# Attention stream: ScalarE exponentiates each head from the score banks, with the row maximum as bias, and sums in the same instructions

## The reference

```python
qp = q @ Wq.T
k, v = jnp.split(latent_kv @ Wkv_expand.T, 2, axis=-1)
scores = jnp.einsum('bhqd,bhkd->bhqk', qh, kh) * inv_sqrt_d
scores = jnp.where(causal, scores, jnp.finfo(scores.dtype).min)
attn = jax.nn.softmax(scores, axis=-1)
out = jnp.einsum('bhqk,bhkd->bhqd', attn, vh)
x = x + jnp.tanh(g_xattn[1]) * (out @ Wout.T)
```

## Time and profile before

| | |
|---|---|
| runs before, median (lowest to highest) | 2217.43 us (2213.9 to 2219.85) |
| the profiled execution | 2218.61 us |
| its span, first to last instruction | 2216.9 us |
| granted TensorE clock, mean | 0.942 |
| TensorE busy (matmuls) | 1946.2 us, 88% |
| VectorE busy | 1421.1 us, 64% |
| ScalarE busy | 959.1 us, 43% |
| GpSimd busy | 509.1 us, 23% |

### The profile page before, as it was taken

How to read it: one execution, slowest core, us unless ns; L and a number is a source line. 1 busy time by engine, 2 the same in 40 slices (tenths; PEclk the granted TensorE clock), 3 DMA queues, 4 the chain that set the end, 5 groups by cost and what they waited for, 6 DMA issues and landing times. The chain is left out here.

```text
span 2216.9 us, 33553 instructions
## 1 busy us (share of the span) xinstructions
PE 1946.2 (88%) x11866; PEld 1541.6 (70%) x11866; DVE 1421.1 (64%) x2759; ACT 959.1 (43%) x1983; POOL 509.1 (23%) x469
## 2 busy tenths in 40 slices
PE   1899999999499999999913999799959989999997
PEld 1677787777377777877711555466639879999996
DVE  3666666676666666666767777366664544666663
ACT  1333344443233333344465333355524425666663
POOL 3211010110311110001022000133220354565553
PEclk9999999999699999999956999899985999999999
DMA  5200000000321001000051000000013147777774
GB/s 135 74 6 33 37 37 37 37 1 1 76 74 38 2 35 37 37 37 1 1 227 63 0 0 0 1 1 1 1 61 98 40 126 166 236 237 232 230 238 99
DMA packets 39530, 154.61 MB, mean 70 GB/s; under 512 B 5472, under 2 KB 12848, under 8 KB 29050
## 3 DMA queue, kind: packets, MB, share of 16 engines
q1 hardware_dynamic: 27170, 128.39, 16.5%
q0 software_dynamic: 11408, 23.37, 5.8%
q10 hardware_dynamic: 840, 1.36, 0.2%
HBM read 132.59 MB, written 20.51 MB: 69 GB/s over the span
## 5 line engine op out<-in xcount | busy, mean ns | idle before, releaser
L608 DVE TENSOR_TENSOR la_q_roped<-banks,la_rope_q 128x400 f32<-128x400 f32 x384 | 197.9, 567 | 45.6 <-PE banks L400 28.6
L555 ACT ACTIVATE la_probs<-banks,la_minus_max 100x361 f32<-100x361 f32 x256 | 145.0, 566 | 157.2 <-DVE la_minus_max L643 157.2
L643 DVE TENSOR_REDUCE la_minus_max<-banks 100x1 f32<-100x361 f32 x256 | 135.7, 530 | 58.9 <-PE banks L426 52.1
L1751 DVE TENSOR_TENSOR ex_weights_low<-ex_raw_weights,ex_weights_high 128x2048 fp32r<-128x2048 f32 x60 | 137.4, 2290 | 51.2 <-ACT ex_weights_high L1658 48.5
L343 POOL TENSOR_TENSOR la_wq_high<-la_weights,zero 128x1024 fp32r<-128x1024 f32 x14 | 26.5, 1894 | 609.6 <-PE banks L372 609.6
L435 PEld LDWEIGHTS banks<-identity,la_probs 100*121 100x121 f32 x768 | 113.4, 184 | 64.3 <-DVE la_probs L650 29.6
L446 PE MATMUL banks<-la_probs_t,la_kv_rows 121*128 121x200 f32 x768 | 151.3, 333 | 0.0
L925 PE MATMUL banks<-qf_sign_weights,qf_x_quant_t 128*100 128x512 bf16 x512 | 122.9, 391 | 32.2 <-DVE qf_hidden L1006 18.1
L573 ACT COPY la_probs_t<-banks 121x300 f32<-121x300 f32 x256 | 106.2, 415 | 96.3 <-PE banks L435 96.3
L2007 POOL TENSOR_TENSOR ex_g_low<-ex_g,ex_g_high 128x256 fp32r<-128x256 f32 (+1 forms) x104 | 86.7, 949 | 232.6 <-ACT ex_g_high L1690 232.1
L435 PE MATMUL banks<-identity,la_probs 100*121 100x100 f32 x768 | 125.6, 272 | 16.0 <-DVE la_probs L650 14.5
(11 more groups left out here) (312 smaller groups left out, 5501.6 us busy)
## 6 DMA issues: line engine op xcount, KB each, us to landing
ex_raw_weights<-w_exp SPq DMA_DIRECT2D x60, 1024.0 KB
la_weights<-w_pack SPq DMA_DIRECT2D x16, 1984.0 KB, 7.8
qf_raw_weights<-w_ffn SPq DMA_DIRECT2D x2, 4096.0 KB
qf_raw_weights<-w_ffn SPq DMA_DIRECT2D x2, 2048.0 KB
out<-ex_block_out POOLq DMA_DIRECT2D x13, 256.0 KB, 4.4
residual<-x SPq DMA_DIRECT2D x1, 3200.0 KB
normed_rows<-ex_xn SPq DMA_DIRECT2D x16, 200.0 KB
out<-residual SPq DMA_DIRECT2D x4, 800.0 KB
```

Of the source, the lines that this page charges most:

```text
L555: act.activation(prob[:, s % 4, 0:L], ps[0:S, s % 2, 0:L], ACT.Exp, bias=nmax[:, s % 4:s % 4 + 1], accum_out=sums[:, s % 4:s % 4 + 1]).the ...
L608: dve.tensor_tensor(roped[:, h, v, c, :].rearrange("p (b s) -> p b s", b=GB), ps[:, B_BANKS[k % 2], 0:NT].rearrange("p (b s) -> p b s", b=GB),
L643: dve.tensor_reduce(nmax[:, s % 4:s % 4 + 1], ps[0:S, s % 2, 0:L], AX.X, ALU.max, negate=True).then_inc(s_max, 1)
L1751: dve.tensor_tensor(wl[:, m, :], raw[:, m, :], wh[:, m, :].bitcast(F32), ALU.subtract).then_inc(w_low[m], 1)
```

## The change

`less_max` becomes `least`: the maximum is taken with its sign turned, and nothing is subtracted. ScalarE's `exp` no longer works in place on SBUF but reads the score banks, one instruction for each head, with the negated maximum of this head as bias and with `accum_out`, which gives the head's row sum. VectorE's sum goes, and `sums` becomes `recips`. TensorE's `scores(j)` waits until the four heads of the item before have been exponentiated.

```diff
@@ TensorE, scores
                     if j >= 1:
-                        pe.wait_ge(s_sub, j)
+                        pe.wait_ge(s_exp, j * HPB)
@@ ScalarE
                 def exp(j):
-                    act.wait_ge(s_sub, j + 1)
-                    act.activation(p[:, j % PR, :], p[:, j % PR, :], ACT.Exp).then_inc(s_exp, 1)
+                    act.wait_ge(s_max, j + 1)
+                    if j >= PR:
+                        act.wait_ge(t_psum, j - PR + 1)
+                    if j >= 4:
+                        act.wait_ge(s_rec, j - 3)
+                    for h in range(HPB):
+                        act.activation(p[:, j % PR, h * S:(h + 1) * S], ps[0:S, h // 2, h % 2 * S:(h % 2 + 1) * S],
+                                       ACT.Exp, bias=mx[:, j % 4, h:h + 1],
+                                       accum_out=sm[:, j % 4, h:h + 1]).then_inc(s_exp, 1)
@@ VectorE
-                def less_max(j):
-                    four = "p b (h s) -> p b h s"
-                    banks = ps[0:S, 0:2, 0:2 * S].rearrange(four, h=2)
+                def least(j):
                     dve.wait_ge(s_psum, j + 1)
-                    dve.tensor_reduce(mx[:, j % 4, :].rearrange("p (b h) -> p b h", b=2), banks, AX.X,
-                                      ALU.max).then_inc(s_max, 1)
-                    dve.wait_ge(s_max, j + 1)
-                    if j >= PR:
-                        dve.wait_ge(t_psum, j - PR + 1)
-                    dve.tensor_tensor(p[:, j % PR, :].rearrange("p (b h s) -> p b h s", b=2, h=2), banks,
-                                      mx[:, j % 4, :].rearrange("p (b h) -> p b h", b=2).unsqueeze(3)
-                                      .to_broadcast([S, 2, 2, S]), ALU.subtract).then_inc(s_sub, 1)
-
-                def sums(j):
-                    dve.wait_ge(s_exp, j + 1)
+                    if j >= 4:
+                        dve.wait_ge(s_exp, (j - 3) * HPB)
+                    dve.tensor_reduce(mx[:, j % 4, :].rearrange("p (b h) -> p b h", b=2),
+                                      ps[0:S, 0:2, 0:2 * S].rearrange("p b (h s) -> p b h s", h=2), AX.X,
+                                      ALU.max, negate=True).then_inc(s_max, 1)
+
+                def recips(j):
+                    dve.wait_ge(s_exp, (j + 1) * HPB)
                     if j >= 4:
                         dve.wait_ge(s_norm, j - 3)
-                    dve.tensor_reduce(sm[:, j % 4, :], p[:, j % PR, :].rearrange("p (h s) -> p h s", h=HPB), AX.X,
-                                      ALU.add).then_inc(s_sum, 1)
-                    dve.wait_ge(s_sum, j + 1)
                     dve.reciprocal(rs[:, j % 4, :], sm[:, j % 4, :]).then_inc(s_rec, 1)
```

More of the change, by code:

```diff
@@ L1123, in causal_attention @@
         v_psum, v_out = sem("v_psum"), sem("v_out")
-        s_psum, s_max, s_sub, s_exp = sem("scores"), sem("scores_max"), sem("scores_less_max"), sem("scores_exp")
-        s_sum, s_rec, s_norm = sem("exp_sum"), sem("rsum"), sem("probs_normed")
+        s_psum, s_max, s_exp = sem("scores"), sem("scores_max"), sem("scores_exp")
+        s_rec, s_norm = sem("rsum"), sem("probs_normed")
         t_psum, t_out = sem("probs_t_psum"), sem("probs_t_out")
@@ L1420, in _ @@
                     if s < ITEMS:
-                        less_max(s)
+                        least(s)
                     if 1 <= s <= ITEMS:
-                        sums(s - 1)
+                        recips(s - 1)
                     piece = front_at(s - 1) if s else None
```

## The result

The changed kernel takes **2265.56 us** (median of four runs, 2260.77 to 2266.58) against 2217.72 before (median, now of four runs): ratio 1.0224, 95% interval 1.0204 to 1.0243. The forecast was 2264, range 2240 to 2282. The profiled execution has a span of 2263.6 us, 46.7 longer than before.

What follows compares the result with a forecast made beforehand. TensorE's work or a 2.26 us loop through the score banks was taken to bound each slot; the profiled 2218.6 us plus 26.3 (loop) plus 20.6 (clock) gave 2265.5, or 2264 in terms of the median, range 2240 to 2282.

Steps and rivals of the forecast that it cites:

- What bounds the kernel: Attention stream: a slot takes the longer of TensorE's own work or the scores-maximum-subtraction loop of 2.26 us.
- Four heads in the loop: ScalarE's four exponentials per slot enter the score-bank loop: 1.45 us together, lengthening it to 3.30 us.
- +26.3 us: Sum over the attention stream's slots of the longer loop's cost, at the clocks of before.
- the fall at 1616.5: Drop of the granted clock already in the stream before the change; 1.6 us, subtracted from the predicted clock loss.
- the clock term: TensorE's longer pauses in the stream make its clock fall to half more often: +20.6 us together.
- The accumulator reads: In ScalarE's heads, `accum_out` adds a 0.19 us read, with the next instruction 0.09 us behind its start.
- The row of the latent attention: Profile row of another stage: exponential of 0.56 us followed after 0.46, then a 0.19 us read; used to price heads.
- Removed work: On VectorE, 64 subtractions (in the loop) and 64 sums (beside the next slot, worth nothing) go: 72 us.
- four times 3.3: Last quarter: one clock fall per round, 2.5 us in the `out` slot plus 0.8 in a plain one.
- The held clock, the first rival: In the stream the clock holds as before, pauses being 2 us at most; only the loop counts, 2244; chance 0.2.
- Heads of another price: ScalarE's heads in the loop: short, about 2238, chance 0.08; long, 2280 without the clock, chance 0.1.
- The router stretch: Behind the stream, 49.6 us of half-clock TensorE work might meet another clock, at most 24.8 us shorter; chance 0.04.

Runs made afterwards that it cites:

- e4: The kernel before, with ScalarE exponentiating in SBUF in four instructions with accum_out and VectorE's sum gone, subtraction and its wait kept: 2227.01 us, ratio 1.0053.
- e2: The kernel before with one wait moved: scores wait for the exponential of the item before, not the subtraction; 2234.77 us, ratio 1.0088.
- e6: The changed kernel with two pairs of score banks in the last quarter, odd items using front's free banks: 2234.20 us, ratio to before 1.0089.
- e7: The kernel before with two pairs of score banks in the last quarter, odd items using front's free banks: 2200.16 us, ratio 0.9938.
- e1: The changed kernel with 292 filler matmuls in TensorE's pauses, in slots without output projection or q piece: 2239.36 us, ratio to before 1.0116.
- e3: The changed kernel without accum_out: four exponentials from the banks, VectorE's sum as before; 2239.02 us, ratio to before 1.0111.
- e8: The kernel of e4 with ScalarE's `high` ahead of the four exponentials of its slot instead of behind them: 2218.12 us, ratio to before 1.0015.

## Why the prediction was right, point by point

**What bounds the kernel.** The reading of a slot as the longer of TensorE's work and one loop through the score banks held in every run but e4, where a chain that it did not have, through ScalarE's `high` and VectorE's `low`, set the slots behind `mix`. e2 moves the loop's end by one wait and gets the worked-out slot, and e6 and e7 open the loop, after which TensorE's own work sets the pace.

**Four heads in the loop.** Predicted 0.34 us a head, 1.45 us for four, a loop of 3.30. Measured 0.33, 1.42 and 3.22 us. The missing 0.08 us lies in three places: the first exponential started at S+1.66, not 1.70, the heads were 0.03 us shorter, and the scores followed 0.14 us behind the last read, not 0.15.

Over the slots the +26.3 us was mis-sized. It still holds the 1.6 us of the fall at 1616.5, which the clock term takes out again, so for a stream at full clock it says 199.2 + 26.3 - 1.6 = 223.9 us. e1 has 221.5, which is 2.4 less. The smaller loop accounts for 0.08 us in each of some 36 slots, 2.9 us. One cost was missed and goes the other way: the first slot takes 3.56 us and not 3.14, since the load of the exponential's table (1.28 us, until S+1.99), which had ended ahead of the subtraction, now stands in the loop.

**The accumulator reads.** By the rule of the Trainium skill's page "ScalarE: Activation LUTs" (section "What ACT_TABLE_LOAD costs"), which names no read, the estimate for four heads was 1.17 us. The traces don't agree: e3, without the reads, measured 1.05 us, and with them it is 1.42. In e3 an exponential is 354 ns long and the next one starts 231 ns behind it, an overlap of 123 ns; in e4, from SBUF and without a bias, the read starts 95 ns before the exponential's end. The same section of the Trainium skill gives 93 ns. The row of the latent attention was the better guide, for the reads' 0.09 us each.

**Removed work.** The sum was said to be worth nothing, as it ran beside the next slot. e8 fits that: sums gone, stream 198.2 against 199.2. It is no proof, since `high` was moved in the same kernel. The subtraction was counted inside the loop, where the heads took its place.

**The clock.** This is the step that decided between 2244 and 2264. Against a stream at full clock the prediction has 20.6 + 1.6 = 22.2 us, and measured are 25.3 (after less e1). So the direction and the mechanism were right, as e1 shows by filling the pauses, and the term was mis-sized in its parts:
- First quarter: 5.8 us where 2.4 was said.
- Second and third: 4.8 and 4.5 where 3.3 each was said. There were two falls in each, not one.
- Fourth: 10.1 where four times 3.3, or 13.2, was said. The clock fell in three rounds, not in four, at +2.4 us for the output slot (6.34 against 3.95; 2.5 was taken) and +0.92 for a plain one (0.8 was taken).

The first quarter was the most under-sized. The same slot with a "k" piece shows why, before, and then after, with the slot in which the clock came back:

```profile
1445.52:1448.99 3.47, 3.47 (x13) 1.83 (x13) 2.83 (x8) 1.83 (x4) 1.58 (x2) 0.50 0.00 0
```

```profile
1449.38:1453.53 4.15, 3.54 (x13) 1.87 (x14) 1.12 (x3) 2.19 (x11) 1.22 (x2) 0.50 0.02 4
...
1457.68:1463.00 5.32, 5.32 (x24) 4.54 (x24) 0.66 (x2) 2.62 (x11) 0.85 (x1) 0.60 0.00 0
```

Before, TensorE filled this slot, and the clock was back at 1449.3. After, the longer loop left a pause in it and in the other slots at half clock (3.61 to 4.15 us), and the clock came back at 1462.0, in a "q" slot that TensorE filled.

The two errors, 2.4 us too much for the loop and 3.1 too little for the clock, nearly cancel, so the total's 1.6 us of distance flatters the parts.

**The held clock, the first rival.** It would have given 2244. The clock fell after 4.10 us with 2.45 busy, and no pause of TensorE in the stream was longer than 2.33 us. The Trainium skill, "TensorE: Matmul & The Clock Gate", Part 1, lets the clock drop when the array has been idle. By the prediction's reading of that rule, under which such pauses would not be enough, the trace disagrees.

**The other rivals.** Heads of another price are excluded by the timeline. The router stretch kept its 64.8 us at half clock.

## What to carry to other kernels

Before an operation is moved to an engine with room, ask which buffer its end releases. A reader of a single pair of banks is in the producer's loop, and there its time lengthens every slot that the loop sets. Outside it, 34 us less on VectorE and 37 us more on ScalarE came out about even where one other instruction was moved out of their way (e8), and cost 10 us where it was not (e4). Then look at the producer's pauses: on TensorE they cost a second time through the clock, here about as much as the loop itself. The cheap remedy was a second pair of banks where some were free (e7), not a different split of the work.

## What the runs showed of the hardware that was not expected

- Filling TensorE's pauses, up to 2 us in a plain slot, with 292 matmuls whose result nobody reads made the changed kernel 26 us faster (2239.36 against 2265.56).
- A 100-column exponential with a bias column, read from the banks, is 351 ns on average in the changed kernel; in SBUF and without a bias (e4) it is 275 ns. No run tells the share of the banks from that of the bias.
- The accumulator read is 214 ns long in the changed kernel against 187 ns in e4, with 0.09 us to the next start in both:

```profile
L1346 ACT ACTIVATION_READ_ACCUMULATOR ca_probs<-banks,ca_maxima 100x1 f32 x256 | 54.7, 214 | 0.0
```

```profile
L1344 ACT ACTIVATION_READ_ACCUMULATOR ca_probs<-ca_probs 100x1 f32 x256 | 47.9, 187 | 0.0
```
